# Half of a plain down product moved ahead of an up product, in the unit that follows the second MLP's plain unit

## Time and profile before

| what | us |
|---|---|
| median of 3 runs | 2070.95 |
| lowest, highest | 2069.89, 2071.57 |
| profiled execution, own time | 2071.11 |
| profiled execution, span | 2069.2 |
| TensorE busy (9500 matmuls) | 2048.5, 99% |
| VectorE busy | 1513.9, 73% |
| ScalarE busy | 1020.3, 49% |
| GpSimd busy | 356.0, 17% |

### The profile page before, as it was taken

The page is one execution under the profiler, slowest core; times in us unless marked ns, Lnnn a source line. Parts: engine busy times, 40 slices in busy tenths (PEclk is TensorE's granted clock), DMA queues, the critical chain, the costliest instruction groups (busy, mean ns, idle before and its releaser), DMA issues.

```text
span 2069.2 us, 27672 instructions
## 1 busy us (share of the span) xinstructions
PE 2048.5 (99%) x9500; PEld 1692.9 (82%) x9500; DVE 1513.9 (73%) x2353; ACT 1020.3 (49%) x1844; POOL 356.0 (17%) x378
## 2 busy tenths in 40 slices
PE   8999999999999999999999999999999999999998
PEld 7888887888788888788888888788888888878886
DVE  6576677888767666888877666788876766768877
ACT  5464454555356444555435544555534645445552
POOL 0011112321101102232000110223100111032211
PEclk9999999999999999999999999999999999999999
DMA  7411211212321121112460112022342011111143
GB/s 286 164 31 41 72 46 62 72 62 107 143 82 40 53 73 50 46 62 72 174 209 31 43 60 74 28 72 72 109 157 93 13 59 52 67 61 61 47 142 93
DMA packets 42377, 169.77 MB, mean 82 GB/s; under 512 B 5625, under 2 KB 9721, under 8 KB 34809
## 3 DMA queue, kind: packets, MB, share of 16 engines
q1 hardware_dynamic: 42096, 167.97, 23.4%
q10 hardware_dynamic: 144, 0.03, 0.0%
HBM read 146.97 MB, written 21.01 MB: 81 GB/s over the span
## 4 chain that ended last, share of the span: by engine, by line
PE 93%; DVE 4%; issue 1%; ACT 1%; DMA 0%; SPq 0%; DVEq 0%; ACTq 0%
PE psum L664 83%; PE psum L989 2%; PE psum L952 2%; PE psum L761 1%; PE psum L739 1%; PE psum L992 1%; PE psum L965 1%; DVE acc L1677 0%; DVE fpart L1408 0%; DVE acc L1674 0%; PE psum L977 0%; DVE wdp L1408 0%; PE psum L955 0%; PE psum L762 0%; PE psum L741 0%
## 5 line engine op out<-in xcount | busy, mean ns | idle before, releaser
L664 PE MATMUL psum<-hs,wd 128*128 128x512 f32 x1920 | 448.2, 390 | 0.5
L664 PEld LDWEIGHTS psum<-hs,wd 128*128 128x128 f32 x1920 | 360.2, 188 | 76.7 <-DVE acc L1677 2.2
L664 PE MATMUL psum<-cop,wsm 128*128 128x512 f32 x1416 | 354.8, 389 | 0.0
L664 PE MATMUL psum<-aop,wsm 128*128 128x512 f32 x1320 | 333.2, 390 | 0.0
L664 PE MATMUL psum<-aop,wsc 128*128 128x512 f32 x1320 | 311.4, 390 | 0.0
L664 PEld LDWEIGHTS psum<-cop,wsm 128*128 128x128 f32 x1416 | 265.9, 188 | 55.0
L664 PEld LDWEIGHTS psum<-aop,wsm 128*128 128x128 f32 x1320 | 247.9, 188 | 51.5
L664 PEld LDWEIGHTS psum<-aop,wsc 128*128 128x128 f32 x1320 | 247.6, 188 | 51.3
L1653 DVE TENSOR_TENSOR acc<-psum,acc 128x1024 f32<-128x1024 f32 x144 | 175.8, 1221 | 87.1 <-PE psum L664 86.9
L1677 DVE TENSOR_TENSOR acc<-psum,acc 128x512 f32<-128x512 f32 x256 | 167.6, 685 | 84.2 <-PE psum L664 84.1
L1408 DVE TENSOR_TENSOR hs<-hs_raw,hs 128x512 fp32r<-128x512 f32 x256 | 178.4, 705 | 43.5 <-ACT hs_raw L1229 43.4
(11 more groups left out here) (191 smaller groups left out, 3027.2 us busy)
## 6 DMA issues: line engine op xcount, KB each, us to landing
w1m<-m_in SPq DMA_DIRECT2D x32, 1024.0 KB, 4.9
w1c<-c_in SPq DMA_DIRECT2D x32, 512.0 KB, 3.5
w<-c_in SPq DMA_DIRECT2D x32, 512.0 KB, 3.6
w<-m_in SPq DMA_DIRECT2D x32, 512.0 KB, 3.5
gains<-roles_in SPq DMA_DIRECT2D x30, 512.0 KB, 4.6
fw<-fused SPq DMA_DIRECT2D x6, 2048.0 KB, 10.2
fused<-fw SPq DMA_DIRECT2D x4, 2048.0 KB, 7.5
xmid<-x SPq DMA_DIRECT2D x4, 2048.0 KB, 6.6
```

Of the source, the lines that this page charges most:

```text
L664: mm = nc.tensor.matmul(out, lhs(a), rhs(b), start=(start and n == 0), stop=(stop and n == total - 1), skip_group_check=reopened)
```

## The change

Three places are touched. On TensorE, in unit 9 alone, two of the four groups of `down(8, 1)` are issued between P2 and P7 instead of behind P7. On ScalarE, in unit 9, the split of down weight P3 and of unit 10's up weight P5 go ahead of H11, and the splits of down weights P1 and P6 go behind the split of the sum P5. On VectorE, in unit 9, `make_z22` goes behind the low parts of unit 10's P1 weight and of down weight P3, and the low parts of down weights P1 and P6 go behind `make_z12`. No instruction is added or removed; nothing changes in other units.

```diff
                     elif u != NG:
                         terms(p, u, P1, P5, P6)
                         down(p, u - 1, 0)
-                        terms(p, u, P2, P7)
-                        down(p, u - 1, 1)
+                        terms(p, u, P2)
+                        if fast(u):
+                            down(p, u - 1, 1, 0, 1)
+                            terms(p, u, P7)
+                            down(p, u - 1, 1, 2, 3)
+                        else:
+                            terms(p, u, P7)
+                            down(p, u - 1, 1)
                         terms(p, u, P4, P3)
...
                 if fast(u):
                     split_part(p, u, P5)
                     weight_part(p, u + 1, P1)
-                    hidden(p, layer, u, H11)
-                    split_part(p, u, P3)
-                    weight_part(p, u + 1, P5)
-                    split_part(p, u, P1, P6)
-                    hidden(p, layer, u, H10)
-                    split_sum(p, u, P5)
+                    if then:
+                        hidden(p, layer, u, H11)
+                        split_part(p, u, P3)
+                        weight_part(p, u + 1, P5)
+                        split_part(p, u, P1, P6)
+                        hidden(p, layer, u, H10)
+                        split_sum(p, u, P5)
+                    else:
+                        split_part(p, u, P3)
+                        weight_part(p, u + 1, P5)
+                        hidden(p, layer, u, H11)
+                        hidden(p, layer, u, H10)
+                        split_sum(p, u, P5)
+                        split_part(p, u, P1, P6)
                     weight_part(p, u + 1, P6)
                     split_sum(p, u, P7, P6)
                     split_part(p, u, P7)
...
                         low_part(p, u, P3)
                     else:
                         low_part(p, u, P5)
-                        make_z22(p, u)
                         weight_part(p, u + 1, P1)
                         low_part(p, u, P3)
+                        make_z22(p, u)
                         add(p, layer, u - 1, 1, *range(KC))
                     weight_part(p, u + 1, P5)
                     if then:
                         fast_add(p, u - 1, P2)
-                    low_part(p, u, P1, P6)
+                        low_part(p, u, P1, P6)
                     hidden_sum(p, u, P5)
                     hidden_sum(p, u, P6)
                     hidden_sum(p, u, P7)
...
                     if then:
                         fast_add(p, u - 1, P4)
                     make_z12(p, u)
+                    if not then:
+                        low_part(p, u, P1, P6)
                     weight_part(p, u + 1, P6)
                     hidden(p, u, H00)
                     hidden(p, u, H11)
```

## The result

The changed kernel takes 2060.70 us (median of 5 runs, 2058.96 to 2061.27) against 2070.95 (5 runs, 2069.89 to 2071.57): ratio 0.9951, 95% interval 0.9937 to 0.9964, so 10.25 us faster; in microseconds the interval is about 7.5 to 13.0. Forecast were 2060.4 us and a range of 2059.0 to 2065.5. The profiled execution took 2058.96, span 2057.1.

A forecast was written before the change was run, and what follows sets the result against it. TensorE, busy 99% of the span, was taken as the bound, its stalls set by VectorE's full queue. Recovering 2.68 us in each of four passes, other terms 0, gave 2071.1 - 10.7 = 2060.4 us, range 2059.0 to 2065.5.

The forecast's parts named there:

- The size: TensorE's stalls in units 9 and 10 of the second MLP all go: 2.68 us a pass, 10.7 us in four.
- TensorE's new order costs nothing: Two new group boundaries around P7 in unit 9: 0 to 0.2 us a pass, taken as 0; a gain excluded.
- The adds sooner, and H10 as the next limit: VectorE's four adds of unit 8 end at 326.95, not 331.01; then it idles until H10, made at 328.95.
- ScalarE's cost of 0: P5 weight's high part, now before H11, waits for P7 until 323.5; H11 waits until 326.26 anyway, so no cost.
- The collision that goes: VectorE's second sum took 1.59 us beside GpSimd's third step, 0.69 free: 0.90 us counted gone.
- the prediction's bound: P1 and P3 low parts fully serialised among GpSimd's steps, 0.69 + 0.42 more: everything ends by 324.95, price 0.
- one free duration: By the exclusion rule, VectorE's 1.59 us sum ends this far behind GpSimd's end: 334.02 + 0.55 = 334.57.
- The tight place: `fast_down(P1)` after `fast_add(P5)`: may start at 342.16, due at 342.32, so 0.16 us to spare.
- VectorE's queue stays the bound: First rival: collisions between H10 and `fast_add(P5)` keep part of the stall; one gives 2063.7, two 2067.7; partial recovery 0.20.
- The change does not touch what it should: Second rival: something else sets `fast_down(9, P5)`'s start, 1.72 us stays, 2067.3 to 2071.1; 0.12 together with two collisions.
- Slower through `make_z22`: Third rival: `make_z22` ends after 325.9 and delays TensorE's P4, each microsecond costing four; 2075.5 if at 329.7; chance 0.06.

The follow-up runs named there:

- the fillers: Changed kernel with one or two added 0.6 us VectorE sums in unit 9, ahead of the low part of unit 10's P6 weight: 2061.64 and 2064.11 us.
- the deferred low parts: Kernel before with only VectorE's low parts of down weights P1 and P6 moved behind `make_z12` in unit 9: 2071.22 us, ratio 1.0000.

## Why the prediction was right, step by step

The size. The 2.68 us a pass were read from starts, not from the waits view, whose rows add up to 7.7 over four passes, 1.9 each. The chain piece gives 2.68 in the first pass. Four passes make 10.7; the medians give 10.25. Right; but it is the traces that confirm 2.68 a pass, the medians alone would allow 1.9 to 3.3.

TensorE's new order costs nothing. Right, by the groups' starts 1.36 apart across both new boundaries, and by the run with this part alone (ratio 1.0001). The prediction did not say that it is also worth nothing; it let the two early groups be among the reasons why the adds run sooner, and gave the change its name by them. In the run without TensorE's move, the fourth add still starts when the last group ends, and that alone sets the time of what follows.

The adds sooner, and H10 as the next limit. Right: 2.09 us idle before H10 (forecast about 2). The step that carries it is the P3 split ahead of H11, shown by the run that moves nothing else. ScalarE's cost of 0 is right too: in the changed kernel the P5 weight's split starts at 322.18 + 1.36 = 323.54, and H11 at 324.90 + 1.36 = 326.26, its old time to the hundredth.

The collision that goes. Right: 0.69 for 1.59, with GpSimd's third step at 326.27 + 1.36 = 327.63, in VectorE's idle stretch. The new collisions were larger than I gave in the term itself: the two low parts took 1.27 and 1.50, not 0.69 and 0.42. That is 1.66 us more on VectorE, where the prediction's bound added 1.11 behind GpSimd's steps; it lies inside the bound all the same, since the last of these steps ends at 322.67 + 1.36 = 324.03 (bound 324.95), and `make_z22` still waited 0.61 us for P7. The trace agrees here too with the rule of the Trainium skill ("SBUF — State Buffer", section "Who interferes with whom") that the one which comes second is blocked for the whole instruction: the low part of 0.42 that took 1.50 from 320.01 ended 0.28 behind GpSimd's step of 319.49 to 321.23. The prediction called such a rest "one free duration"; in both cases it is nearer to the distance between free starts (0.28 against 0.34, 0.55 against 0.60) than to the rows' free durations of 0.42 and 0.69.

The tight place. Right: 0.19 us of margin against 0.16, confirmed from outside by the fillers: 0.60 us more made it 0.40 late, 1.20 made it 1.00 late.

The rivals. "VectorE's queue stays the bound" did not come, but was 0.19 us away, as the fillers show: 0.40 and 1.00 of their 0.60 and 1.20 us reached TensorE. "The change does not touch what it should" is refuted: with the low sum at 331.65 the stall that the profile called "issue" is gone. "Slower through `make_z22`" is a real mechanism with its price shown, at an order that this change does not have. That a full recovery could be read off a margin of 0.16 us rests on how well the durations repeat: the forecast starts of VectorE's three instructions were met within 0.03 us.

Not tried: VectorE's move of `make_z22` behind the P3 low part without ScalarE's move. There ScalarE's H11 would wait for `make_z22` and, standing ahead of the P3 split, hold back what VectorE waits for: both would stand still. That is read from the code only.

## What to carry to other kernels

When an engine's queue has been full since some instruction, look for what that first instruction waited for: here one 0.4 us copy in the wrong place on ScalarE held VectorE's four adds for 4.1 us (331.01 against 326.95 in the same time base), and its move gave all but 0.14 us a pass of the gain by itself, and all of it together with that of one weight split. Take the size of a stall from the starts of the rows and a free pitch, and test each part of a change that has several, since the part that names it may be worth nothing. In this kernel the stall in front of the full queue only moved when the queue's order was changed, and went when the queue's work started sooner.

## What the runs showed of the hardware beyond that

The profiled executions of before and after differ by 12.15 us, the chain of the four passes by 10.7. Of the rest, 1.36 lies ahead of unit 1 of the first MLP, in code that the change does not touch. The windows view of both kernels over 30 to 36 us (busy time and instructions of each engine, PEclk the granted clock) shows it. First before, then after:

```profile
30.00:36.00 6.00, 4.04 (x11) 3.20 (x12) 6.00 (x7) 4.72 (x6) 0.00 (x0) 0.72 0.40 127
```

```profile
30.00:36.00 6.00, 3.79 (x17) 3.15 (x18) 6.00 (x7) 4.89 (x6) 0.00 (x0) 1.00 0.45 127
```

TensorE had been idle for 2.9 and 3.0 us before it started a step of 96 matmuls in this stretch, before and after:

```profile
31.96 23.65 PE L664 MATMUL psum<-fpart 128*128 128x512 f32 x96 [2.93 <-DVE fw L1408]
```

```profile
32.21 22.04 PE L664 MATMUL psum<-fpart 128*128 128x512 f32 x96 [3.01 <-DVE fw L1422]
```

Once it restarted at a granted clock that averages 0.72, partly at the lower level of 1.2 GHz, and did 11 matmuls there; once at 1.00, at 2.4 GHz all through, with 17. The 96 matmuls took 23.65 and 22.04 us; less the 0.25 by which the step began later, that is the 1.36. In other executions, among them the one with the deferred low parts (0.63, then 0.80 in the next six microseconds), they took up to 24.87. So 1.6 to 2.8 us of an execution's time are settled there, by something that these runs don't name. The timed runs scatter by the same order (1.7 us before and 2.3 after in five runs each, 4.0 in fifteen runs of the kernel before); whether this step makes that scatter is not shown, since only the profiled executions have a trace. A comparison of two single executions of this kernel carries it.
